# End of an edge stage: pieces of the node chunks placed by tables of steps, two edges' node rows fetched by SyncE

## The chip, the cores and the metric

The kernel runs on one core of one Trainium2 chip. The metric is the device time of one execution in microseconds (us). Engines are written as in the profile: PE (matrix multiplication, with PEld for its weight loads), DVE (VectorE), ACT (ScalarE), POOL (GpSimd) and SP (SyncE, here only an issuer of transfers).

## What is computed

Four graph layers over 1250 nodes with 512 features, each followed by a layer norm. The last one is the one that matters here; it is the only layer that reads an attribute for every one of the 21250 edges:

```python
msg = jax.nn.relu(x[src] + edge_attr)
agg = jax.ops.segment_sum(msg, dst, num_segments=x.shape[0])
h = x + agg
h = jax.nn.relu(h @ W1 + b1) @ W2 + b2
h = x + h
mean = h.mean(axis=0)
var = h.var(axis=0)
h = (h - mean) * jax.lax.rsqrt(var + BN_EPS) * gamma + beta
```

Edges are sorted by `dst`, so the sums of the first nodes are ready long before those of the last.

## The kernel before

**Groups.** The edge stage of the last layer works through 42 groups of 512 edges (`NG = 42`), four tiles of 128 edges each; the last group has 258 edges, so its tiles 2 and 3 hold one edge each. For a group g, SP loads the attributes into one of nine slots `ea`, and POOL gathers the node rows of the sources into one of three slots `xg` (`gather`, L490), one indirect transfer per tile, each of which waits until DVE has read that tile three groups earlier. DVE adds `xg` to `ea` (`add_rows`, L1020, four instructions) and writes the window matrix `hot_w` (L1023). ACT applies the relu (`rectify`, L657; L659 and L660 for the last group). PE multiplies (`scatter`, L1361, eight matmuls).

**Pairs.** Two groups make a pair m. After the second scatter ACT copies PSUM to `zn` (`evac_pair`, L667), PE transposes it (`turn`, L1371), and DVE adds four windows into the node sums `x3T` (`add_pair`, L1035). The places of the windows depend on the data: ahead of its wait for PE, `add_pair` loads four registers from SBUF (L1028).

**Chunks.** As soon as the pairs that touch a range of nodes are in, this range goes through the two matrix products. There are seven chunks q; chunks 2 to 4 are 180 nodes wide, 5 is 120 and 6 is 134. Each has four stages of four instructions or groups of 16 quarter pieces: `pre_chunk` on PE (L1382), `hidden_chunk` on ACT (L675), `out_chunk` on PE (L1393) and `add_chunk` on DVE (L1043, and bn_stats at L1046, which waits for L1043's semaphore). A piece is numbered 0 to 3, and pieces 0, 1 and 2, 3 are placed together as two halves. PSUM has two buffers for each product: `out_chunk` piece c waits until DVE has added piece c-2, and `pre_chunk` until ACT has read piece f-2. `hidden_chunk(q, 0)` waits until all of `out_chunk` of chunk q-1 is done, since `h1` has one buffer.

**Order.** Each engine runs its instructions strictly in the order of the program, and that order is written by a loop over steps g, one per group, that continues for `LATE = 9` steps behind the last group. In a step each engine does its work on group g, then the pair that is due, then the chunk pieces whose step it is, by `at_chunk(q)`, which is a number of steps behind the last group of the chunk. `pair_at(m)` is 2m+3 for m from 16 on, so pair 18 is added at step 39, pair 19 at 41, and pair 20, the last, at 43. Pieces of chunk 6 come last on all engines; its `pre_chunk` waits for every window of every pair. Behind it stand the statistics over all nodes, the normalisation and the last transposes and stores, which all need every chunk.

Of the kernel before, what the change touches and what calls it, by code (L numbers as in the profile page):

```python
# [27 lines left out]
P = 128  # L28
N = 1250
# [3 lines left out]
KC = D // P  # L33
NT = (N + P - 1) // P
# [22 lines left out]
FLAG_AT = 33  # L57
ACT_LOS = (2, 1, 2, 1)
NPAIR = NG // 2
LATE = 9  # L60
TURN_X = (18, 23)
GROUP_CUTS = (8, 16, 22, 28, 34, 38, NG)
GNODES, SLACK = 30, 24
NODE_CUTS = [0] + [GNODES * g - SLACK for g in GROUP_CUTS[:-1]] + [N]
NCUT = len(NODE_CUTS) - 1
SOON = 16
CMAX = max(b - a for a, b in zip(NODE_CUTS, NODE_CUTS[1:]))
XTILES = 4
TLAG = 3
# [1 line left out]
LN_SETS = ((0, 2), (2, 4), (4, 6), (6, 8), (8, 9), (9, 10))  # L71
PE_SUMS = (2, 3, 5, 6, 8, 9)
EPS = 1e-5
assert CS * (NCH - 1) + CH == N and NCODE <= 512 and NG == 2 + NT * HOTS and NG % 2 == 0 and NB * EW * 2 == P and not any(g % 2 for g in GROUP_CUTS)
assert BLOCK_SPAN * GE + 1 <= 4096 and BE < LAST < GE and (TPG * 2 + 3) * NG <= 512


# [4 lines left out]
def gnn_kernel(nc, x, src, dst, edge_attr, w01, b01, w02, b02, w11, b11, w12, b12, w2, b2,  # L82
               w31, b31, w32, b32, gamma, beta, out, x3_dram):
    with ExitStack() as ctx:
# [18 lines left out]
        def sem(name):  # L103
            return ctx.enter_context(nc.semaphore(name))
# [174 lines left out]
        ea_loaded = [sem(f"ea_loaded{i}") for i in range(RING)]  # L279
        xg_loaded = [[sem(f"xg_loaded{i}_{r}") for r in range(TPG)] for i in range(XRING)]  # L280
        idx_seen = sem("idx_seen")
        add_done, relu_done, win_ready = sem("add_done"), sem("relu_done"), sem("win_ready")
        scat_done, zn_ready, turn_done, win_added = sem("scat_done"), sem("zn_ready"), sem("turn_done"), sem("win_added")
        fix_x, fix_e, fix_msg, fix_done, fix_added = (sem("fix_x"), sem("fix_e"), sem("fix_msg"), sem("fix_done"), sem("fix_added"))
# [25 lines left out]

            return edge_attr[g * GE:(g + 1) * GE, :].rearrange("(b p r) d -> p b (r d)", b=NB, r=2)

        def at_chunk(q):

            return GROUP_CUTS[q] + (1 if NCUT - 3 <= q < NCUT - 1 else 3)

        def pair_at(m):

# [31 lines left out]
        def _(sp):  # L350
# [23 lines left out]
            def load(g):  # L374
                s = g % RING
                if g >= RING:
                    sp.wait_ge(scat_done, g - RING + 1)
                if g < NG - 1:
                    sp.dma_start(ea[s][:, :, :].rearrange("p (b r) d -> p b (r d)", b=NB), ea_rows(g)).then_inc(ea_loaded[s], 16)
                    return  # L380
                e0 = g * GE
                sp.dma_start(ea[s][:, 0:2, :].rearrange("p r d -> p (r d)"),
                             edge_attr[e0:e0 + BE, :].rearrange("(p r) d -> p (r d)", r=2)).then_inc(ea_loaded[s], 16)
                sp.dma_start(ea[s][0:LAST_P, 2:4, :].rearrange("p r d -> p (r d)"),
                             edge_attr[e0 + BE:e0 + BE + 2 * LAST_P, :].rearrange("(p r) d -> p (r d)", r=2)).then_inc(ea_loaded[s], 16)
# [7 lines left out]
            sp.wait_ge(y_done, 3 * NT)  # L393
            for g in range(early, NG):
                load(g)

            for j in range(NT):
                sp.wait_ge(x_ready, 3 * NT + j + 1)
# [6 lines left out]
        def _(pool):  # L405
# [77 lines left out]

            def gather(g):
                slot = g % XRING
                for r in range(TPG):
                    if g >= XRING:
                        pool.wait_ge(add_done, TPG * (g - XRING) + r + 1)
                    n = max(tile_rows(g, r), 2)
                    pool.indirect_dma_start(out=xg[0:n, slot, r, :], out_offset=None, in_=x3_dram[:, :],  # L490
                                            in_offset=bass.IndirectOffsetOnAxis(ap=srcT_i[0:n, r, g:g + 1], axis=0)).then_inc(xg_loaded[slot][r], 16)

            for g in range(NG):
                gather(g)
# [3 lines left out]
        def _(act):  # L498
# [170 lines left out]
            def hidden_chunk(q, f):  # L669

                n = NODE_CUTS[q + 1] - NODE_CUTS[q]
                act.wait_ge(pre_done, q * KC + f + 1)
                if q and f == 0:
                    act.wait_ge(h2_done, q * KC)
                act.activation(h1[:, f, 0:n], ps[:, 2 + f % 2, 0:n], ACT.Relu, bias=cols[:, 1, f:f + 1]).then_inc(h1_ready, 1)  # L675

            for g in range(NG + LATE):
                if g < NG:
                    rectify(g)
                if g % 2 == 0 and 2 <= g <= NG:  # L680
                    evac_pair(g // 2 - 1)
                for q in range(NCUT):
                    if g in (at_chunk(q) + 1, at_chunk(q) + 2):
                        for f in halves(g - at_chunk(q) - 1):
                            hidden_chunk(q, f)

            act.wait_ge(bn_step, 2 * KC)
            act.activation(bn_t[:, 0, :], bn_mv[:, :, 1:2].rearrange("p c a -> p (c a)"), ACT.Sqrt, bias=eps_s[:, 0:1]).then_inc(bn_sq, 1)
# [22 lines left out]
        def _(dve):  # L711
# [301 lines left out]
            def add_rows(g):  # L1013

                s, slot = g % RING, g % XRING
                dve.wait_ge(ea_loaded[s], 16 * (g // RING + 1) + 16 * (g == NG - 1))
                for r in range(TPG):
                    dve.wait_ge(xg_loaded[slot][r], 16 * (g // XRING + 1))
                    n = tile_rows(g, r)
                    dve.tensor_tensor(ea[s][0:n, r, :], ea[s][0:n, r, :], xg[0:n, slot, r, :], ALU.add).then_inc(add_done, 1)  # L1020
                if g >= RING:
                    dve.wait_ge(scat_done, g - RING + 1)
                dve.tensor_tensor(hot_w[:, s, :, :], iota_n[:, 0:EW].unsqueeze(1).to_broadcast([P, TPG, EW]),  # L1023
                                  relwT[:, :, g:g + 1].to_broadcast([P, TPG, EW]), ALU.is_equal).then_inc(win_ready, 1)
# [22 lines left out]
                if q == NCUT - 1:  # L1047
                    ins.then_inc(bn_step, 1)

            for g in range(NG + LATE):  # L1050
                if g < NG:
                    add_rows(g)
                for m in range(NPAIR):
                    if g == pair_at(m):
                        add_pair(m)
                for q in range(NCUT - 1):
                    if g in (at_chunk(q) + 5, at_chunk(q) + 7):
                        for cc in halves((g - at_chunk(q) - 5) // 2):
                            add_chunk(q, cc)

            for cc in range(KC):
                add_chunk(NCUT - 1, cc)
                dve.wait_ge(bn_step, 2 * cc + 1)
# [53 lines left out]
        def _(pe):  # L1117
# [276 lines left out]
                                    start=(k == 0), stop=(k == KC - 1))  # L1394
                ins.then_inc(h2_done, 1)

            for g in range(NG + LATE):
                if g < NG:
                    scatter(g)
                if g % 2 == 0 and 2 <= g <= NG:  # L1400
                    turn(g // 2 - 1)
                for q in range(NCUT):
                    if g in (at_chunk(q), at_chunk(q) + 1):
                        for f in halves(g - at_chunk(q)):
                            pre_chunk(q, f)
                    if g in (at_chunk(q) + 3, at_chunk(q) + 5):
                        for cc in halves((g - at_chunk(q) - 3) // 2):
                            out_chunk(q, cc)

            for j in range(NT):  # L1410
                for i, (n0, n1) in enumerate(BN_PARTS):
# [44 lines left out]
```

## Time and profile before

| | us |
|---|---|
| median of 3 runs | 590.97 |
| lowest, highest | 589.76, 594.39 |
| the profiled execution, time | 594.86 |
| the profiled execution, span from first to last instruction | 593.2 |
| PE busy | 495.4 (84%) |
| DVE busy | 395.8 (67%) |
| POOL busy | 302.5 (51%) |
| ACT busy | 251.9 (42%) |

The time of an execution is a little above its span (1.66 us here). Shares of busy time are averages over stages with different limits: the edge stage fills about the stretch from 310 to 560 us, and the change touches its last 35 us. Starts in the rows below are microseconds from the beginning of the span. In a timeline several like instructions that follow each other are one row (x16 is sixteen), and an idle time before a row stands in brackets with what ended it. PE's successive matmuls overlap a little, so the distance from one row's start to the next is slightly below the row's duration.

### The profile page before, as it was taken

What the parts mean: (1) busy time and instruction counts of PE and PEld (TensorE: products, weight loads), DVE (VectorE), ACT (ScalarE), POOL (GpSimd) and SP (SyncE); (2) the same over time, 40 slices, a digit from 0 to 9 for tenths busy, and PEclk for the clock granted to TensorE, in tenths of its full rate; (3) what the DMA queues carried; (4) which work ended last, traced back from release to release, by engine and by line L of the source; (5) the groups of instructions that cost most, each with busy time, mean ns of one, the idle gap of its engine ahead of it and who ended that gap; (6) DMA issues with size and microseconds to landing.
All of it is one profiled execution on the core that took longest, in us unless ns stands there. A gap on an engine that the chain in (4) does not pass through costs nothing.

```text
span 593.2 us, 7933 instructions
## 1 busy us (share of the span) xinstructions
PE 495.4 (84%) x2461; PEld 345.9 (58%) x2461; DVE 395.8 (67%) x894; ACT 251.9 (42%) x435; POOL 302.5 (51%) x328
## 2 busy tenths in 40 slices
PE   4999999999999998999992546578569876889875
PEld 2544459997899964899881101134235543465775
DVE  7999986768848959111672646565694776787375
ACT  7677751121285126410124424434435343444335
POOL 8999838301004005850004777777777777773000
PEclk9999999999999999999996567779979899899979
DMA  7900000000000400000947899999999999973004
GB/s 263 270 1 0 2 2 1 0 0 2 0 1 2 143 0 0 2 0 0 371 178 299 299 395 371 385 396 389 393 388 358 399 397 399 354 193 95 1 1 173
DMA packets 35604, 102.64 MB, mean 173 GB/s; under 512 B 6635, under 2 KB 7277, under 8 KB 35562
## 3 DMA queue, kind: packets, MB, share of 16 engines
q1 hardware_dynamic: 22150, 58.51, 26.4%
q0 software_dynamic: 13344, 43.53, 20.4%
q8 instruction: 20, 0.33, 0.2%
q14 instruction: 22, 0.18, 0.1%
q10 hardware_dynamic: 68, 0.09, 0.0%
HBM read 96.99 MB, written 5.12 MB: 172 GB/s over the span
## 4 chain that ended last, share of the span: by engine, by line
PE 42%; POOL 15%; DMA 14%; DVE 14%; issue 7%; ACT 5%; DVEq 3%; ACTq 0%; SPq 0%; POOLq 0%
DMA xg<-x_dram,srcT_i 13%; PE ps L1200 12%; POOL xg L490 11%; PE ps L1239 10%; PE ps L1212 7%; POOL hot_lo L426 4%; DVE ea L1020 3%; DVE hot_code L815 3%; PE ps L1268 2%; PE ps L1361 2%; PE ps L1382 2%; PE ps L1393 2%; ACT countsT L592 2%; DVEq L1028 2%; PE ps L1155 1%
## 5 line engine op out<-in xcount | busy, mean ns | idle before, releaser
L490 POOL DMA_INDIRECT xg<-x_dram,srcT_i x168 | 171.8, 1022 | 109.3 <-DMA x_dram<-xn 57.5
L1361 PE MATMUL ps<-ea,hot_w 128*32 128x512 f32 x336 | 94.5, 706 | 68.0 <-ACT ea L657 67.9
L1020 DVE TENSOR_TENSOR ea<-ea,xg 128x512 f32<-128x512 f32 x168 | 108.8, 689 | 35.1 <-DMA xg<-x_dram,srcT_i 34.7
L657 ACT ACTIVATE ea<-ea 128x2048 f32<-128x2048 f32 x41 | 78.3, 1910 | 110.3 <-DVE ea L1020 110.3
L1361 PEld LDWEIGHTS ps<-ea,hot_w 128*32 128x32 f32 x336 | 17.6, 120 | 123.5 <-ACT ea L657 72.9
L426 POOL TENSOR_SCALAR hot_lo<-iota_n,src_loT 128x128 bf16<-128x128 f16 x105 | 65.9, 644 | 4.8 <-PE ps L1155 3.9
L1035 DVE TENSOR_TENSOR x3T<-x3T,ps 128x128 f32 x84 | 24.3, 289 | 45.0 <-issue 26.0
L815 DVE TENSOR_SCALAR hot_code<-iota_c,codeT 128x380 bf16<-128x380 f16 x168 | 49.2, 352 | 2.4 <-issue 0.8
L1382 PEld LDWEIGHTS ps<-x3T,w_s 128*128 128x128 f32 x224 | 35.9, 200 | 9.6 <-issue 5.8
L1177 PE MATMUL ps<-w_s,xT 128*128 128x512 f32 (+1 forms) x80 | 41.1, 595 | 0.0
L1382 PE MATMUL ps<-x3T,w_s 128*128 128x180 f32 (+4 forms) x224 | 39.6, 332 | 1.1 <-ACT h L675 1.1
L1155 PE MATMUL ps<-hot_code,hot_lo 128*128 128x380 bf16 x168 | 35.9, 337 | 5.2 <-DVE hot_code L815 2.6
L1393 PE MATMUL ps<-h,w_s 128*128 128x180 f32 (+4 forms) x224 | 36.6, 318 | 0.8 <-ACT h L675 0.5
L1155 PEld LDWEIGHTS ps<-hot_code,hot_lo 128*128 128x128 bf16 x168 | 15.6, 100 | 34.3 <-DVE hot_code L815 19.0
L1393 PEld LDWEIGHTS ps<-h,w_s 128*128 128x128 f32 x224 | 33.7, 190 | 1.7 <-ACT h L675 0.7
L574 ACT ACTIVATE std<-mv,eps_s 128x1 f32<-128x1 f32 x30 | 8.8, 294 | 59.8 <-DVE mv L906 59.8
L1212 PE MATMUL ps<-counts,xs_lo 128*128 (+1 forms) x120 | 32.9, 355 | 1.3 <-POOL xs_lo L450 1.3
L1212 PE MATMUL ps<-counts,xs_hi 128*128 (+1 forms) x120 | 33.1, 357 | 0.0
L445 POOL TENSOR_TENSOR g_lo<-g_f,g_hi 128x256 fp32r<-128x256 f32 (+1 forms) x10 | 7.3, 734 | 49.3 <-ACT g_f L608 49.3
L971 DVE TENSOR_TENSOR z_lo<-ps,z_hi 128x418 f32 x12 | 6.6, 589 | 38.0 <-ACT z_hi L641 38.0
L450 POOL TENSOR_TENSOR xs_lo<-xs_f,xs_hi 128x512 fp32r<-128x512 f32 (+1 forms) x10 | 12.7, 1275 | 37.5 <-ACT xs_hi L630 37.5
L826 DVE TENSOR_TENSOR counts<-ps,counts 128x380 f32 x42 | 22.8, 543 | 3.0 <-PE ps L1155 2.7
(180 smaller groups left out, 950.6 us busy)
## 6 DMA issues: line engine op xcount, KB each, us to landing
ea<-in_edge_attr_dram SPq DMA_DIRECT2D x41, 1024.0 KB, 9.7
w_s<-in_L_gnn_W_dram SPq DMA_DIRECT2D x5, 1024.0 KB, 8.8
xg<-x_dram,srcT_i POOLq DMA_INDIRECT x168, 7.4
xn<-in_x_dram SPq DMA_DIRECT2D x3, 768.0 KB, 8.4
x_dram<-xn SPq DMA_DIRECT2D x9, 256.0 KB
out_dram<-xn SPq DMA_DIRECT2D x9, 256.0 KB
w_s<-in_L_gnn_W_dram SPq DMA_DIRECT2D x2, 512.0 KB, 11.5
b_b<-in_L_gnn_b_dram SPq DMA_DIRECT2D x3, 256.0 KB, 10.0
```

The lines of the kernel that those rows point to most:

```text
L426: ins = pool.tensor_scalar(hot_lo[:, slot, r, :], iota_n[:, 0:P], src_loT[:, r, g:g + 1], None, ALU.is_equal)
L490: pool.indirect_dma_start(out=xg[0:n, slot, r, :], out_offset=None, in_=x3_dram[:, :], in_offset=bass.IndirectOffsetOnAxis(ap=srcT_i[0:n, ...
L657: act.activation(ea[s][:, :, :], ea[s][:, :, :], ACT.Relu).then_inc(relu_done, 1)
L815: ins = dve.tensor_scalar(hot_code[:, slot, r, :], iota_c[:, :], codeT[:, r, g:g + 1], None, ALU.is_equal)
L1020: dve.tensor_tensor(ea[s][0:n, r, :], ea[s][0:n, r, :], xg[0:n, slot, r, :], ALU.add).then_inc(add_done, 1)
L1155: ins = pe.matmul(ps[:, 4 + slot, 0:NCODE], hot_lo[:, slot, r, :], hot_code[:, slot, r, :], start=(r == 0), stop=(r == TPG - 1))
L1200: ins = pe.matmul(ps[:, cc, 0:CH], part[0:rows(j), j, P * cc:P * cc + P], rhs[0:rows(j), j, n], start=(first and m == 0), stop=(last and m ...
L1212: ins = pe.matmul(ps[:, cc, 0:CH], part[0:rows(j), j, P * cc:P * cc + P], rhs[0:rows(j), j, n], start=(j == 0 and part is parts[0]), stop= ...
L1239: ins = pe.matmul(ps[0:rows(j), 4 + n % 2, :], act_t[:, k, P * j:P * j + rows(j)], w[:, k, :], start=(m == 0), stop=(m == len(pairs) - 1))
L1361: ins = pe.matmul(ps[at_w:at_w + EW, 4 + g // 2 % 2, :], hot_w[:, g % RING, 2 * b + r, :], ea[g % RING][:, 2 * b + r, :], start=(r == 0), ...
L1382: ins = pe.matmul(ps[:, 2 + f % 2, 0:n1 - n0], w31_s[:, k, P * f:P * f + P], x3T[:, k, n0:n1], start=(k == 0), stop=(k == KC - 1))
L1393: ins = pe.matmul(ps[:, cc % 2, 0:n], w32_s[:, k, P * cc:P * cc + P], h1[:, k, 0:n], start=(k == 0), stop=(k == KC - 1))
```

## The change

Four things are changed.

1. `at_chunk` and `LATE` go; tables of steps say at which step each half of chunks 0 to 5 runs on each engine. Chunk 6 runs behind the loop, on each engine. Compared step by step, PE's first product and ACT's pieces stay at the steps they had. PE's second product moves for chunk 4 from steps 38 and 40 to 37 and 39, and for chunk 5 from 42 and 44 to 41 and 42: its first half now stands ahead of the transposes of the last pair. DVE's sums move for chunk 3 (second half) from step 38 to 37, for chunk 4 from 40 and 42 to 39 and 41, where the second half now stands ahead of pair 19, and for chunk 5 the first half now stands ahead of the last pair, where it stood behind it.
2. In a PE step in which both occur, `out_chunk` now precedes `pre_chunk`.
3. In the last group, tiles 2 and 3 (one edge each) are no longer gathered by POOL. SP loads two registers with the source numbers, waits until DVE has read these tiles of group 38, and issues two transfers of one row each. This stands behind all attribute loads and ahead of the stores of the output.
4. DVE adds the last group's tiles in the order 2, 3, 0, 1.

```diff
-LATE = 9
+PRE_AT = ((11, 12), (19, 20), (25, 26), (31, 32), (35, 36), (39, 40))
+HIDDEN_AT = ((12, 13), (20, 21), (26, 27), (32, 33), (36, 37), (40, 41))
+OUT_AT = ((14, 16), (22, 24), (28, 30), (34, 36), (37, 39), (41, 42))
+ADD_AT = ((16, 18), (24, 26), (30, 32), (36, 37), (39, None))
-        def at_chunk(q):
-
-            return GROUP_CUTS[q] + (1 if NCUT - 3 <= q < NCUT - 1 else 3)
+        def pieces(steps, g):
+
+            return [(q, 2 * i + c) for q, at_step in enumerate(steps) for i in range(2) if at_step[i] == g for c in range(2)]
...
+            ends = [sp.value_load(srcT_i[0:1, r, NG - 1:NG], min_val=0, max_val=N - 1) for r in (2, 3)]
+            sp.wait_ge(x3_stored, 16 * NT)
+            for r, end in zip((2, 3), ends):
+                sp.wait_ge(add_done, TPG * (NG - 1 - XRING) + r + 1)
+                sp.dma_start(xg[0:1, (NG - 1) % XRING, r, :], x3_dram[bass.ds(end, 1), :]).then_inc(end_loaded[r - 2], 16)
...
-                for r in range(TPG):
+                for r in range(TPG if g < NG - 1 else 2):
...
-            for g in range(NG + LATE):
-                if g < NG:
-                    rectify(g)
-                if g % 2 == 0 and 2 <= g <= NG:
+            for g in range(NG):
+                rectify(g)
+                if g % 2 == 0 and g >= 2:
                     evac_pair(g // 2 - 1)
...
+                for q, f in pieces(HIDDEN_AT, g):
+                    hidden_chunk(q, f)
+            evac_pair(NPAIR - 1)
+            for f in range(KC):
+                hidden_chunk(NCUT - 1, f)
...
-                for r in range(TPG):
-                    dve.wait_ge(xg_loaded[slot][r], 16 * (g // XRING + 1))
+                for r in range(TPG) if g < NG - 1 else (2, 3, 0, 1):
+                    if g == NG - 1 and r >= 2:
+                        dve.wait_ge(end_loaded[r - 2], 16)
+                    else:
+                        dve.wait_ge(xg_loaded[slot][r], 16 * (g // XRING + 1))
...
-            for g in range(NG + LATE):
-                if g < NG:
-                    add_rows(g)
-                for m in range(NPAIR):
+            for g in range(NG):
+                add_rows(g)
+                if g == NG - 1:
+                    for cc in halves(1):
+                        add_chunk(NCUT - 3, cc)
+                for m in range(NPAIR - 1):
                     if g == pair_at(m):
                         add_pair(m)
...
+                for q, cc in pieces(ADD_AT, g):
+                    add_chunk(q, cc)
+            for cc in halves(0):
+                add_chunk(NCUT - 2, cc)
+            add_pair(NPAIR - 1)
+            for cc in halves(1):
+                add_chunk(NCUT - 2, cc)
             for cc in range(KC):
                 add_chunk(NCUT - 1, cc)
...
-            for g in range(NG + LATE):
+            for g in range(NG + 1):
                 if g < NG:
                     scatter(g)
-                if g % 2 == 0 and 2 <= g <= NG:
+                if g % 2 == 0 and g >= 2:
                     turn(g // 2 - 1)
...
+                for q, cc in pieces(OUT_AT, g):
+                    out_chunk(q, cc)
+                for q, f in pieces(PRE_AT, g):
+                    pre_chunk(q, f)
+            for f in range(KC):
+                pre_chunk(NCUT - 1, f)
+            for cc in range(KC):
+                out_chunk(NCUT - 1, cc)
```

## Rows read from the trace of the kernel before

**Rows 1.** The page's tenths in 40 slices: busy PE, granted clock, DMA.
```profile
PE   4999999999999998999992546578569876889875
...
PEclk9999999999999999999996567779979899899979
DMA  7900000000000400000947899999999999973004
```

**Rows 2.** Windows: busy time (count) of PE, PEld, DVE, ACT, POOL; clock, DMA share, GB/s.
```profile
500.00:505.00 5.00, 4.32 (x24) 2.81 (x24) 2.28 (x4) 2.15 (x2) 3.78 (x5) 1.00 1.03 399
...
531.00:560.20 29.20, 26.59 (x167) 17.98 (x167) 18.97 (x49) 13.25 (x17) 8.04 (x8) 1.00 0.24 68
```

**Rows 3.** Timeline of PE: start, us, engine, line, operation [idle before].
```profile
534.21 1.91 PE L1361 MATMUL ps<-ea,hot_w 128*32 128x512 f32 x8
536.58 1.91 PE L1361 MATMUL ps<-ea,hot_w 128*32 128x512 f32 x8 [0.46 <-ACT ea L657]
538.42 0.66 PE L1371 MATMUL ps<-ident,zn 128*128 128x128 f32 x4
538.91 2.61 PE L1393 MATMUL ps<-h,w_s 128*128 128x180 f32 x16
541.45 1.91 PE L1361 MATMUL ps<-ea,hot_w 128*32 128x512 f32 x8
543.29 2.04 PE L1382 MATMUL ps<-x3T,w_s 128*128 128x120 f32 x16
545.27 1.91 PE L1361 MATMUL ps<-ea,hot_w 128*32 128x512 f32 x8
...
550.72 2.04 PE L1382 MATMUL ps<-x3T,w_s 128*128 128x120 f32 x16 [0.51 <-ACT h L675]
552.84 1.91 PE L1361 MATMUL ps<-ea,hot_w 128*32 128x512 f32 x8
555.44 0.66 PE L1371 MATMUL ps<-ident,zn 128*128 128x128 f32 x4 [0.69 <-ACT zn L667]
555.93 1.94 PE L1393 MATMUL ps<-h,w_s 128*128 128x120 f32 x16
558.19 2.02 PE L1393 MATMUL ps<-h,w_s 128*128 128x120 f32 x16 [0.31 <-DVE hT L1043]
560.04 3.83 PE L1382 MATMUL ps<-x3T,w_s 128*128 128x134 f32 x32
```

**Rows 4.** Timeline of DVE in the same stretch.
```profile
539.22 1.55 DVE L1035 TENSOR_TENSOR x3T<-x3T,ps 128x128 f32 x4 [2.27 <-PE ps L1371]
540.69 2.49 DVE L1020 TENSOR_TENSOR ea<-ea,xg 128x512 f32<-128x512 f32 x4
...
543.30 0.40 DVE L1043 SCALAR_TENSOR_TENSOR hT<-ps,cols,hT 128x180 f32<-128x180 f32 x1
...
544.69 2.47 DVE L1020 TENSOR_TENSOR ea<-ea,xg 128x512 f32<-128x512 f32 x4
...
550.68 0.35 DVE L1046 BATCH_NORM_STATS2 bn_st<-hT 128x6 f32<-128x180 f32 x1
556.24 1.55 DVE L1035 TENSOR_TENSOR x3T<-x3T,ps 128x128 f32 x4 [5.21 <-PE ps L1371]
...
560.62 0.29 DVE L1046 BATCH_NORM_STATS2 bn_st<-hT 128x6 f32<-128x120 f32 x1
```

**Rows 5.** Timeline of ACT in the same stretch: the last relus.
```profile
543.22 1.91 ACT L657 ACTIVATE ea<-ea 128x2048 f32<-128x2048 f32 x1 [4.40 <-DVE ea L1020]
...
550.80 1.06 ACT L659 ACTIVATE ea<-ea 128x1024 f32<-128x1024 f32 x1
```

**Rows 6.** L1028 from 552 to 556.2 us, DVE's sequencer: ns min/median/max, starts.
```profile
L1028 DVEq TENSOR_LOAD <-base_i x2: 300/301/302, 551.9 to 552.6; - x2
L1028 DVEq FUSED_REGOPS  x2: 183/183/183, 552.3 to 552.9; - x2
```

**Rows 7.** Timeline of POOL: the last gather, of one edge.
```profile
540.31 0.87 POOL L490 DMA_INDIRECT xg<-x_dram,srcT_i  x1 [0.30 <-issue]
```

**Rows 8.** Gathers from 535 to 546 us: issue to landing.
```profile
DMA to landing us min/median/max: 2.1/3.5/3.9
```

**Rows 9.** Timeline of PE: two scatters behind an idle stretch.
```profile
512.77 4.86 PE L1361 MATMUL ps<-ea,hot_w 128*32 128x512 f32 x16 [2.39 <-ACT ea L657]
```

More of the change, by code:

```diff
@@ L73 @@
 EPS = 1e-5
-assert CS * (NCH - 1) + CH == N and NCODE <= 512 and NG == 2 + NT * HOTS and NG % 2 == 0 and NB * EW * 2 == P and not any(g % 2 for g in GROUP_CUTS)
+assert LAST_P == 1 and LAST_R == 0 and CS * (NCH - 1) + CH == N and NCODE <= 512 and NG == 2 + NT * HOTS and NG % 2 == 0 and NB * EW * 2 == P and not any(g % 2 for g in GROUP_CUTS)
 assert BLOCK_SPAN * GE + 1 <= 4096 and BE < LAST < GE and (TPG * 2 + 3) * NG <= 512
@@ L281, in gnn_kernel @@
         idx_seen = sem("idx_seen")
+        end_loaded = [sem(f"end_loaded{i}") for i in range(2)]
         add_done, relu_done, win_ready = sem("add_done"), sem("relu_done"), sem("win_ready")
@@ L485, in gather @@
                 slot = g % XRING
-                for r in range(TPG):
+                for r in range(TPG if g < NG - 1 else 2):
                     if g >= XRING:
                         pool.wait_ge(add_done, TPG * (g - XRING) + r + 1)
-                    n = max(tile_rows(g, r), 2)
-                    pool.indirect_dma_start(out=xg[0:n, slot, r, :], out_offset=None, in_=x3_dram[:, :],
-                                            in_offset=bass.IndirectOffsetOnAxis(ap=srcT_i[0:n, r, g:g + 1], axis=0)).then_inc(xg_loaded[slot][r], 16)
+                    pool.indirect_dma_start(out=xg[:, slot, r, :], out_offset=None, in_=x3_dram[:, :],
+                                            in_offset=bass.IndirectOffsetOnAxis(ap=srcT_i[:, r, g:g + 1], axis=0)).then_inc(xg_loaded[slot][r], 16)
             for g in range(NG):
@@ L675, in hidden_chunk @@
                 act.activation(h1[:, f, 0:n], ps[:, 2 + f % 2, 0:n], ACT.Relu, bias=cols[:, 1, f:f + 1]).then_inc(h1_ready, 1)
-            for g in range(NG + LATE):
-                if g < NG:
-                    rectify(g)
-                if g % 2 == 0 and 2 <= g <= NG:
+            for g in range(NG):
+                rectify(g)
+                if g % 2 == 0 and g >= 2:
                     evac_pair(g // 2 - 1)
[L682 to L685, printed above, removed]
+                for q, f in pieces(HIDDEN_AT, g):
[3 more added lines that the diff above has]
+                hidden_chunk(NCUT - 1, f)
             act.wait_ge(bn_step, 2 * KC)
@@ L1048, in add_chunk @@
                     ins.then_inc(bn_step, 1)
-            for g in range(NG + LATE):
-                if g < NG:
-                    add_rows(g)
-                for m in range(NPAIR):
+            for g in range(NG):
[4 more added lines that the diff above has]
+                for m in range(NPAIR - 1):
                     if g == pair_at(m):
                         add_pair(m)
[L1056 to L1059, printed above, removed]
+                for q, cc in pieces(ADD_AT, g):
[5 more added lines that the diff above has]
+                add_chunk(NCUT - 2, cc)
             for cc in range(KC):
@@ L1395, in out_chunk @@
                 ins.then_inc(h2_done, 1)
-            for g in range(NG + LATE):
+            for g in range(NG + 1):
                 if g < NG:
                     scatter(g)
-                if g % 2 == 0 and 2 <= g <= NG:
+                if g % 2 == 0 and g >= 2:
                     turn(g // 2 - 1)
[L1402 to L1408, printed above, removed]
+                for q, cc in pieces(OUT_AT, g):
[6 more added lines that the diff above has]
+                out_chunk(NCUT - 1, cc)
             for j in range(NT):
```

## The prediction

> **What bounds the kernel now.** I read the page's slices first. PE is busy in eight or nine tenths of every slice but the first up to slice 21 (311 us); then comes the edge stage, where the DMA engines stand at nine tenths through slices 24 to 35 (341 to 519 us), PE at four to nine [rows 1]. So over most of the edge stage transfers set the pace, and the reader should see that this ends before the stage does: the DMA digit falls to 7, 3, 0, while PE's is 8, 9, 8. The change acts there. The windows give the two regimes in numbers: from 500 to 505 us the DMA engines are full (share 1.03), while from 531 to 560.2 us, with the clock at its higher level throughout, they are at 0.24 and PE is busy 26.59 of 29.20 us [rows 2]. The last 29 us of the stage are therefore bound by PE, and all that can be won there by any order of the same work is 29.20 - 26.59 = 2.6 us. The timeline of PE names these gaps: 0.46 us ahead of a scatter, 0.51 ahead of a first product, 0.69 for the copy of the last pair and 0.31 behind it [rows 3], and crumbs.
>
> Counting backwards, the scatters at 534.21, 536.58, 541.45, 545.27 and 552.84 are those of groups 37 to 41 [rows 3]. The end is set thus: the last scatter, the transposes of pair 20, both halves of chunk 5's second product, and chunk 6's first product at 560.04. Everything behind it (33 us) is a chain of its own that the change leaves as it is. So the question is one number: when does chunk 6's first product start? It needs PE to be free and the four window sums of pair 20, which now end at 556.24 + 1.55 = 557.8, 2.2 us early [rows 4].
>
> **The parts without a price.** (a) POOL's last gather is issued at 540.31 for 0.87 us, with 0.30 between gathers, and gathers land 2.1 to 3.9 us after issue [rows 7, 8]: by 545.1 us at the latest. DVE begins the last group's adds at 544.69 and needs the fourth tile three adds of about 0.62 us later, and then waits for nothing [rows 4]. Taking two gathers off POOL ends its work 2 x (0.87 + 0.30) = 2.3 us sooner, but it hides: the adds stand behind DVE's other work. I price it at 0; the bound on the gain is 2.3 us, if in some run the gathers were last. (b) SP has issued all attribute loads by then. It may fetch tile 2 when DVE has added tile 2 of group 38, about 534 us. With a gather's 3.9 us that is 538, nine us before the adds that I find below; 0, and only a fetch of over 12 us would cost. What stands behind it on SP are the output stores, 40 us later. (c) ACT's order is unchanged, and up to step 36 so is everybody's. (d) The new order of the last adds is the same work: 2.47 us [rows 4]. (e) Chunk 3's late sums move ahead of the adds of group 38 (1.4 us, the distance from 543.30 to 544.69 [rows 4]), which ACT at that time cannot take up sooner anyway.
>
> **The order replayed.** I take durations as the distances between starts in the rows, and keep the waits of the code. All in us. PE's scatter costs 1.84, its transposes 0.49, a half of the second product 2.54 at 180 nodes, and a half of the first at 120 nodes 1.98 [rows 3].
> - Scatter 37 stays at 534.21. Chunk 4's second product, first half, now follows at 536.05 and fills the gap of 0.46. Scatter 38: 538.59. Transposes of pair 18: 540.43, two us later than 538.42 before. Scatter 39: 540.92, and PE is free at 542.76.
> - DVE's sums of pair 18 follow the start of the transposes by 0.8 (539.22 - 538.42): 541.23 instead of 539.22. Behind them now stand the first sums of chunk 4, at 541.23 + 1.47 = 542.70 (1.47 is the distance 540.69 - 539.22), and only then group 40's adds, at 544.09 instead of 540.69 [rows 4]. This is the first cost: the adds of group 40 are 3.4 us later.
> - Chunk 4's second half on PE needs the buffer that DVE's first sum frees, 542.70 + 0.40 = 543.10; it starts at about 543.25 and ends at 545.79, having waited 0.5. The first half of chunk 5's first product: until 547.77.
> - Group 40's adds end at 544.09 + 2.49 = 546.58, its relu at 546.62 + 1.91 = 548.53 [rows 4, 5]. Scatter 40 starts at 548.58; PE has stood still for 0.8. Transposes at 550.42, chunk 5's first product, second half, from 550.91, and scatter 41 at 552.89. The relu of the last group is no hindrance: adds 546.74 to 549.21, relu from 549.6 to 551.6.
> So the last scatter starts at 552.89 where it started at 552.84. The gaps removed (0.46, 0.51, which was ACT waiting for chunk 4's second product) come back as 0.5 and 0.8.
>
> **Behind the last scatter.** Let T be the end of it, 554.73 (before: 554.68). Before, chunk 6 started at T + 5.36 [rows 3]. Now PE does chunk 5's first half at once, which hides the copy of the pair (0.69 saved), then the transposes, then the second half: PE is free at about T + 4.65, so PE alone would gain 0.7. But DVE has the half chunk's sums ahead of the last pair, and with them its register loads. Chunk 5's last bn_stats of a half starts 2.43 behind the start of that half's product (560.62 - 558.19 [rows 3, 4]). Then the loads: before, those of pair 20 began with the bn_stats ahead of them (550.68 [rows 4]) and the last began at 552.6, its register operation at 552.9 for 0.18 [rows 6]. Spacing 0.63, end 553.1, and some 0.15 to the first sum: 2.6 from that bn_stats' start to the first sum. Before, all of it lay in DVE's idle 5.21 us ahead of 556.24 [rows 4]; this cover is gone. First window sum at T + 2.43 + 2.6 = T + 5.05, the last ends 1.55 later [rows 4], T + 6.6, and chunk 6 starts at T + 6.7 = 561.4. That is 561.4 - 560.04 = +1.35. It is a wait of 2 us of PE, in place of one of 0.69 and one of 0.31.
>
> Could the loads run earlier? The bound below is that they are done in time: chunk 6 at T + 4.65 = 559.4, -0.65. The rows speak for the upper value: the loads of pair 20 began with the bn_stats that waits on a semaphore, not before, though DVE had idled. The Trainium skill (Advanced Engine Details and Errata, Engine Queue Depths) gives VectorE a queue of 8 instructions; if that let the four loads pass the four queued instructions of the half chunk, which wait for PE, the cost would vanish and the sum would be the -0.65 above. The trace does not agree for a queue headed by a wait.
>
> **Sum.** 0 for POOL, SP and ACT, +0.05 up to the last scatter, +1.3 behind it: +1.35. Against the profiled execution's own 594.86 this is 596.2. That execution lies above the median of the three runs; the same addition to the median gives 590.97 + 1.35 = 592.3.
>
> **Rivals.**
> - *DVE is ahead (faster).* The loads are hidden (-0.65), and the two new gaps of 0.5 and 0.8 shrink, since they hang on DVE too. All together -0.65 - 1.3 = -1.95: 589.0. For it: DVE idles 2.27 and 5.21 us in this stretch [rows 4], so the work fits. Against: the order of the program. It decides where the loads are done by T + 2.9, when the pair's transposes are. Chance 0.25.
> - *The clock falls (slower).* At about 512 us PE had idled 2.39 us, and two scatters took 4.86 where two distances of 1.84 are 3.7 [rows 9, 3]: +1.2. If the new gap of 2 us ahead of chunk 6 does the same, its price is at least this 1.2 and at most a doubling of the 3.83 of chunk 6's first product. 592.3 + 1.2 to 3.8: 593.5 to 596.1. Against: the gap is shorter. The Trainium skill (TensorE: Matmul & The Clock Gate, Why this matters for your kernels) advises against idle gaps between bursts of matmuls and names one longer than mine as harmful; by it nothing is added here. No row shows a fall behind a gap of 2 us. Chance 0.12.
> - *Nothing shows.* The moved work and the gather's 2.3 cancel, within 0.5 of before: 591.0. Chance 0.12.
> - *SP's fetch is late.* Place: DVE's first adds of group 41. It decides from 12 us of fetch on, three times what rows 8 show. Price: what exceeds it, shared with nothing: 593 and more. Chance 0.03.
>
> **How the numbers follow.** The forecast has 0.48 and its own range is 591.3 to 593.7 (each distance in the replay is good to about 0.1, some ten of them, and the load time to 0.5). The bounds above take the range to 588.8 (the faster rival) and 595.8 (most of the clock's). One per cent is 5.9 us, about what a measurement of this kernel can tell from no change; no case but sums of mishaps gets there, and the largest conceivable gain is 2.6 from PE's gaps and 2.3 from POOL. Faster by over 1%: 0.04, within: 0.91, slower: 0.05; what is not in the cases above I put there.
>
> **What would show it.** In the timeline of PE the order from 536 on: L1393 directly behind scatter 37, no 0.46; a gap of about 0.8 ahead of a scatter, ended by ACT's relu; and one of 1.5 to 2 ahead of the L1382 x32, ended by DVE's L1035. On DVE: L1028's last loads behind the L1046 of 120 nodes, and group 40's adds behind L1043. POOL: two gathers fewer, DVE without a wait for transfers in the last group. The prediction is wrong if chunk 6's first product starts without a gap, if its distance to the last scatter is below 7 us (before: 7.2), or if PE shows more than about 4 us of gaps between 531 and the start of chunk 6.

## The result, and the profile after

| | before | changed |
|---|---|---|
| median of 13 runs, us | 592.50 | 596.15 |
| lowest, us | 589.76 | 592.51 |
| ratio to before (95% interval) | | 1.0045 (1.0025 to 1.0065) |
| the profiled execution, time, us | 594.86 | 594.07 |
| its span, us | 593.2 | 592.4 |

The change costs 0.45% of 592.5, or 2.7 us (1.5 to 3.9). The ratio leaves out executions more than 1.5% above the fastest of the same kernel, here one of 2575.59 us of the changed kernel, whose cause no run shows. The sign is the forecast one and the size is twice the 1.35 us forecast. The median of 596.15 counts that one execution; over the other twelve it is 595.39. The kernel before, too, measures 1.5 us higher in 13 runs than in the three on which the prediction stood; on the median of those three the ratio gives 593.6.

The two profiled executions hide the loss: the changed one is even 0.8 us shorter. They differ ahead of the changed stretch, where the transfers of the edge stage set the pace (368 and 383 GB/s before, 374 and 391 now, in the windows from 330 to 400 and 400 to 460 us), so they have to be laid over each other at a mark behind that part. I use the second half of chunk 4's first product, the last one on 180 nodes (531.58 before, 528.46 now), and call the distance from it the *distance*. The timeline of PE in the changed kernel:

```profile
528.46 2.71 PE L1398 MATMUL ps<-x3T,w_s 128*128 128x180 f32 x16 [0.56 <-ACT h L684]
531.10 1.91 PE L1377 MATMUL ps<-ea,hot_w 128*32 128x512 f32 x8
532.94 2.71 PE L1409 MATMUL ps<-h,w_s 128*128 128x180 f32 x16
535.57 1.91 PE L1377 MATMUL ps<-ea,hot_w 128*32 128x512 f32 x8
...
540.23 2.68 PE L1409 MATMUL ps<-h,w_s 128*128 128x180 f32 x16 [0.31 <-DVE hT L1055]
542.74 1.94 PE L1398 MATMUL ps<-x3T,w_s 128*128 128x120 f32 x16
545.54 1.91 PE L1377 MATMUL ps<-ea,hot_w 128*32 128x512 f32 x8 [0.86 <-ACT ea L666]
...
549.75 1.91 PE L1377 MATMUL ps<-ea,hot_w 128*32 128x512 f32 x8
551.59 2.04 PE L1409 MATMUL ps<-h,w_s 128*128 128x120 f32 x16
553.48 0.60 PE L1387 MATMUL ps<-ident,zn 128*128 128x128 f32 x4
553.91 1.94 PE L1409 MATMUL ps<-h,w_s 128*128 128x120 f32 x16
558.33 5.59 PE L1398 MATMUL ps<-x3T,w_s 128*128 128x134 f32 x32 [2.47 <-DVE x3T L1047]
```

Against [rows 3] the reader should see three things. The small gaps have changed places: 0.46 and 0.51 are gone, 0.31 and 0.86 are there instead, and the last scatter stands at distance 21.29 where it stood at 21.26. Behind it PE runs without a gap for three pieces and then stands still for 2.47 us until DVE's sums of the last pair (L1047) are in; chunk 6 starts at distance 29.87 instead of 28.46. And the same 32 matmuls of chunk 6 then take 5.59 us instead of 3.83.

The timeline of DVE for the same end, from pair 18's sums (538.21) on; group 40's adds are at 541.06:

```profile
538.21 1.55 DVE L1047 TENSOR_TENSOR x3T<-x3T,ps 128x128 f32 x4 [4.20 <-PE ps L1387]
...
541.06 2.48 DVE L1032 TENSOR_TENSOR ea<-ea,xg 128x512 f32<-128x512 f32 x4
...
550.05 1.56 DVE L1047 TENSOR_TENSOR x3T<-x3T,ps 128x128 f32 x4 [2.32 <-issue]
552.78 0.34 DVE L1055 SCALAR_TENSOR_TENSOR hT<-ps,cols,hT 128x120 f32<-128x120 f32 x1 [1.18 <-PE ps L1409]
...
553.68 0.34 DVE L1055 SCALAR_TENSOR_TENSOR hT<-ps,cols,hT 128x120 f32<-128x120 f32 x1 [0.23 <-PE ps L1409]
554.05 0.29 DVE L1058 BATCH_NORM_STATS2 bn_st<-hT 128x6 f32<-128x120 f32 x1
556.72 1.55 DVE L1047 TENSOR_TENSOR x3T<-x3T,ps 128x128 f32 x4 [2.38 <-issue]
```

and the register loads of the last pair, on DVE's sequencer, with their first and last start:

```profile
L1040 DVEq TENSOR_LOAD <-base_i x4: 301/301/308, 554.1 to 555.9; - x4
L1040 DVEq FUSED_REGOPS  x4: 183/186/190, 554.4 to 556.3; - x4
```

DVE's idle 2.38 us ahead of the window sums waits for no engine: the profile calls it "issue", and the loads fill it, from the start of bn_stats at 554.05 on. The pair's transposes had been done at 554.1. Pair 19's sums at 550.05 stand behind four exposed loads as well (2.32 us), and PE shows no gap for it: DVE's next sums wait 1.18 us for PE anyway. Before, the four sums waited 5.21 us for PE, and the loads lay in that time [rows 4, 6].

### The profile page after: what moved, and what is told of

It is laid out like the page before. It is cut to its first block, busy times and chain, and to the rows that moved or that the text cites. A ratio compares the mean times of both kernels' runs of the same rounds, so it can differ in the third digit from the quotient of the medians.

```text
span 592.4 us, 7946 instructions
## 1 busy us (share of the span) xinstructions
PE 493.2 (83%) x2461; PEld 344.1 (58%) x2461; DVE 395.2 (67%) x894; ACT 251.6 (42%) x435; POOL 299.8 (51%) x326
## 4 chain that ended last, share of the span: by engine, by line
PE 42%; POOL 19%; DVE 14%; issue 10%; DMA 8%; ACT 4%; DVEq 2%; ACTq 0%
POOL xg L499 19%; PE ps L1216 12%; PE ps L1255 10%; DMA xg<-x_dram,srcT_i 7%; PE ps L1228 7%; DVE hot_code L824 5%; PE ps L1284 2%; PE ps L1398 2%; PE ps L1377 2%; ACT countsT L601 2%; DVE counts L835 2%; PE ps L1171 2%; PE ps L1409 1%; DVE stats L913 1%; DVE ea L1032 1%
## 5 line engine op out<-in xcount | busy, mean ns | idle before, releaser
L499 POOL DMA_INDIRECT xg<-x_dram,srcT_i x166 | 168.2, 1013 | 107.8 <-DMA x_dram<-xn 57.5
L1032 DVE TENSOR_TENSOR ea<-ea,xg 128x512 f32<-128x512 f32 (+1 forms) x168 | 108.7, 689 | 33.7 <-DMA xg<-x_dram,srcT_i 33.4
L1047 DVE TENSOR_TENSOR x3T<-x3T,ps 128x128 f32 x84 | 24.2, 288 | 46.3 <-issue 32.9
```

What stands on the lines that cost most here:

```text
L499: pool.indirect_dma_start(out=xg[:, slot, r, :], out_offset=None, in_=x3_dram[:, :], in_offset=bass.IndirectOffsetOnAxis(ap=srcT_i[:, r, g ...
```

## The experiments

All distances come from one profiled execution each; they repeat to 0.1 us as long as the product at the mark itself runs at the higher clock (2.71 us), while whole executions scatter by several. The kernels marked as having slower transfers ran beside a kernel before of 642 to 645 us, with wide intervals; the others beside one of 592 to 594 us. The last number of these two rows, GB/s in the edge stage, shows it, first for the changed kernel, then for the first of the slower ones. Ratios hold within a comparison. "Changed" was compared with the kernel before in a comparison of its own; the kernels from "loads early" to "busy gap" shared another.

```profile
400.00:460.00 60.00, 45.29 (x205) 23.61 (x205) 37.15 (x82) 26.37 (x23) 46.49 (x45) 0.94 1.02 391
```

```profile
400.00:460.00 60.00, 37.88 (x170) 21.40 (x168) 35.89 (x78) 19.74 (x18) 39.90 (x40) 0.82 0.93 340
```

| kernel | last scatter | chunk 6 starts | its first product takes | ratio (95%) |
|---|---|---|---|---|
| before | 21.26 | 28.46 | 3.83 | 1 |
| changed | 21.29 | 29.87 | 5.59 | 1.0045 (1.0025 to 1.0065) |
| loads early | 21.29 | 27.38 | 3.92 | 0.9951 (0.9927 to 0.9974) |
| chunk 5 only | 21.28 | 29.85 | 3.92 | 1.0022 (1.0001 to 1.0043) |
| SP only | 21.27 | 28.46 | 3.83 | 0.9987 (0.9966 to 1.0007) |
| busy gap | 21.28 | 29.86 | 3.92 | 1.0006 (0.9985 to 1.0026) |
| loads and adds early, slower transfers | 20.37 | 26.45 | 3.92 | 0.9926 (0.9871 to 0.9981) |
| loads doubled, slower transfers | 21.30 | 32.32 | 5.58 | 1.0112 (1.0001 to 1.0223) |
| loads and adds early, third time | 20.35 | 26.44 | 3.92 | 0.9964 (0.9941 to 0.9987) |

The kernels that the table leaves out had a late mark or no ratio, or repeat a row; they follow in the text.

**The loads taken from under the wait.** `window_places(m)` is the four loads taken out of `add_pair`. The places of the last pair are loaded directly behind the last group's adds, the sums stay where the change has them:

```diff
             for g in range(NG):
                 add_rows(g)
                 if g == NG - 1:
+                    last_places = window_places(NPAIR - 1)
                     for cc in halves(1):
                         add_chunk(NCUT - 3, cc)
...
-            add_pair(NPAIR - 1)
+            add_pair(NPAIR - 1, last_places)
```

> The changed kernel, with the four register loads of the last pair taken from the pair's own place to a place directly behind the last group's adds, where 2.5 us of adds cover them. Theory A (the loads stand exposed between chunk 5's first sums and the last pair, and the gap they make lets the clock fall): the gap of 2.47 us ahead of chunk 6's first product goes to at most 0.3, that product takes 3.83 us instead of 5.59, the distance from chunk 4's last first-product half to chunk 6's start is 27.3 us (changed kernel 29.87, before 28.46), and the time is 0.996 to 1.000 of before. Theory B (the loss sits further up, in the adds of group 40 that stand behind pair 18): the gap closes but the time stays near 1.003. Theory C (the window sums themselves stand too late, not their loads): the gap stays above 1.5 us.

Its timeline of PE:

```profile
551.33 1.91 PE L1382 MATMUL ps<-ea,hot_w 128*32 128x512 f32 x8
553.17 2.04 PE L1414 MATMUL ps<-h,w_s 128*128 128x120 f32 x16
555.06 0.60 PE L1392 MATMUL ps<-ident,zn 128*128 128x128 f32 x4
555.49 1.94 PE L1414 MATMUL ps<-h,w_s 128*128 128x120 f32 x16
557.42 3.92 PE L1403 MATMUL ps<-x3T,w_s 128*128 128x134 f32 x32
```

No gap, and full clock. Chunk 6 starts at 27.38 as expected, 2.49 us sooner than in the changed kernel and 1.08 sooner than before. Theories B and C fall: nothing but four loads was moved, and the kernel is faster than both, by a little more than I had expected (0.9951, where 0.996 was the end of my range; the interval holds it). Not all of it is explained: against the kernel before the ratio says 2.9 us (1.5 to 4.3), the distance only 1.08, and behind the start of chunk 6 this trace shows no gain. In the same trace the four loads start from 542.9 to 544.7 us, beside group 40's adds and ahead of the last group's adds (545.25), behind which they stand in the program.

**One part of the change alone.** In the kernel before, only chunk 5's first half goes ahead of the last pair:

```diff
-                    if g in (at_chunk(q) + 3, at_chunk(q) + 5):
+                    if g in (at_chunk(q) + (2 if q == NCUT - 2 else 3), at_chunk(q) + 5):
...
+                if g == pair_at(NPAIR - 1):
+                    for cc in halves(0):
+                        add_chunk(NCUT - 2, cc)
```

> The kernel before, with one thing of the change: the first half of chunk 5's second product ahead of the last pair's transposes on PE, and its sums ahead of the last pair's sums on DVE. All else is as before. Theory A: this alone makes a gap of 2 to 2.5 us ahead of chunk 6, whose start moves from 28.46 to 29.8 us behind chunk 4's last first-product half; +1.35 us without a fall of the clock, about +3.1 with one; time 1.002 to 1.005 of before. Theory B: 1.000, since the adds of group 40 are not delayed here.

```profile
550.18 1.91 PE L1364 MATMUL ps<-ea,hot_w 128*32 128x512 f32 x8
...
558.75 3.92 PE L1385 MATMUL ps<-x3T,w_s 128*128 128x134 f32 x32 [2.47 <-DVE x3T L1035]
```

The gap is there to the hundredth, 2.47 us, and chunk 6 starts at 29.85. So the whole shift comes from this one exchange, none of it from the tables for chunks 3 and 4 or from SP. But the product behind the gap took 3.92 us: in this execution the clock did not fall. The ratio, 1.0022, is the forecast's 1.35 us almost exactly (0.22% of 594 is 1.3), but its interval reaches from 0.1 to 2.6 us, so this closeness proves nothing, and it does not tell this kernel from the changed one.

**SP's rows alone.** The kernel before with points 3 and 4 of the change:

```diff
-                for r in range(TPG):
+                for r in range(TPG if g < NG - 1 else 2):
...
+                sp.dma_start(xg[0:1, (NG - 1) % XRING, r, :], x3_dram[bass.ds(end, 1), :]).then_inc(end_loaded[r - 2], 16)
```

> The kernel before, with only the other part of the change: tiles 2 and 3 of the last group fetched by SP, two gathers fewer on POOL, and the order 2, 3, 0, 1 of the last adds. Theory A: POOL ends 2.3 us sooner, nothing on PE, DVE or ACT moves by more than 0.2 us; 0.999 to 1.001 of before. Theory C' (the transfers matter): faster by up to 2.3 us, 0.996, or slower if DVE waits for SP's rows.

SP's two transfers and POOL's last gather, from the timelines of the two engines:

```profile
532.06 0.77 SPq L402 DMA_DIRECT2D xg<-x_dram  x2
...
536.37 0.95 POOL L496 DMA_INDIRECT xg<-x_dram,srcT_i  x1 [0.30 <-issue]
```

POOL is done at 537.3 instead of 541.2, by the mark 3.6 us sooner (2.3 had been expected), and no distance on PE moves by more than 0.01 us. The ratio 0.9987 can't be told from 1. This part is hidden, as forecast.

**The gap filled with useless work.** In the changed kernel, PE transposes the unit matrix into a free bank:

```diff
+            for i in range(12):
+                pe.transpose(ps[:, 5, 0:P], ident[:, :], ident[:, :])
             for f in range(KC):
                 pre_chunk(NCUT - 1, f)
```

> The changed kernel, with 12 transposes of the unit matrix into a PSUM bank that is free then, between chunk 5's last product and chunk 6's first: work that nobody needs, about 1.5 us, inside the gap of 2.47 us. If the fall of the clock is caused by the idle gap, chunk 6's first product takes 3.83 us instead of 5.59 at an unchanged start, and the time is 1.000 to 1.003 of before where the changed kernel has 1.0045. If the clock falls on its own account, the product stays at 5 us or more and the ratio at 1.0045.

```profile
556.97 1.47 PE L1423 MATMUL ps<-ident 128*128 128x128 f32 x12
559.60 3.92 PE L1398 MATMUL ps<-x3T,w_s 128*128 128x134 f32 x32 [1.16 <-DVE x3T L1047]
```

Chunk 6 starts at 29.86 as in the changed kernel, with 1.16 us of standstill instead of 2.47, and its product takes 3.92 us. The ratio is 1.0006 where the changed kernel has 1.0045, 2.3 us less. That fits a clock that falls because PE stands still, but it is not shown: the intervals touch (up to 1.0026, down from 1.0025), and the two ratios come from different comparisons. In this one the kernel with chunk 5's half alone has the same gap without the useless work; its 1.0022 can't be told from 1.0006, and its product took 3.92 us too.

**The adds of group 40 first.** DVE idles 4.20 us in the changed kernel ahead of pair 18's sums. Group 40's adds go there, and the places of the last three pairs are loaded early:

```diff
             for g in range(NG):
-                add_rows(g)
+                if g != NG - 2:
+                    add_rows(g)
+                if g == NG - 3:
+                    places[g // 2 - 1] = window_places(g // 2 - 1)
+                    add_rows(NG - 2)
                 if g == NG - 1:
+                    for m in (NPAIR - 2, NPAIR - 1):
+                        places[m] = window_places(m)
```

> The changed kernel with the loads of the last three pairs moved ahead, as in the early-loads kernel, and also group 40's adds ahead of pair 18's sums and chunk 4's first sums, into DVE's idle 4.2 us there. Theory A: the gap of 0.86 us ahead of scatter 40 goes as well; the last scatter starts 20.4 us behind chunk 4's last first-product half (before 21.26, changed 21.29, early loads 21.29), chunk 6's first product at 26.5 (28.46, 29.87, 27.38), the time is 0.995 to 0.998 of before, and below that of the early-loads kernel by about 0.9 us. Rival: the adds of group 40 wait for their gathers or delay pair 18, and nothing is won over the early-loads kernel.

The last scatter is at 20.37 and chunk 6 at 26.45, both as expected, two us ahead of before; the gap of 0.86 is gone. The ratio was 0.9926 with slower transfers. It ran twice more:

> The kernel with early loads and early adds again, since its first runs fell on a chip with slower transfers and gave a wide interval. Theory A: last scatter at 20.4 us, chunk 6 at 26.5 us behind chunk 4's last first-product half, no gap ahead of chunk 6, 0.993 to 0.998 of before. Rival: the early-loads kernel's 0.9951 was mostly luck of the clock, and this one comes to 0.998 or more.

0.9919 (0.9877 to 0.9961), distances 20.36 and 26.45, transfers slow again.

> The kernel with early loads and early adds a third time, to see its ratio where transfers are as fast as in the first comparison (before at about 592 us). Theory A: the distances are 20.4 and 26.5 us again, and the ratio is 0.993 to 0.997; on a chip with slower transfers (before at about 643 us) again 0.992 with a wide interval.

```profile
544.47 1.91 PE L1388 MATMUL ps<-ea,hot_w 128*32 128x512 f32 x8
...
548.67 1.91 PE L1388 MATMUL ps<-ea,hot_w 128*32 128x512 f32 x8
...
554.76 3.92 PE L1409 MATMUL ps<-x3T,w_s 128*128 128x134 f32 x32
```

0.9964 with the fast transfers: 2.1 us (0.8 to 3.5) below before, 4.8 below the changed kernel by the two ratios, which come from two comparisons. That it is also faster than the kernel with early loads alone (0.9951) is not shown; the 0.9 us between them are visible in the distances, not in the times.

**The loads doubled.** In the changed kernel the four loads ahead of the last pair are done twice:

```diff
+            for j in range(4):
+                dve.value_load(base_i[0:1, 1 + j % NB, NG - 2 + j // NB:NG - 2 + j // NB + 1], min_val=0, max_val=N - EW)
             add_pair(NPAIR - 1)
```

> The changed kernel with the four register loads ahead of the last pair's sums done twice, the first time for nobody. If the gap ahead of chunk 6 consists of these loads, it goes from 2.47 us to 5.0, chunk 6 starts at 32.4 us behind chunk 4's last first-product half (changed kernel 29.87), and the time is 1.007 to 1.012 of before. If the loads lie beside something else that ends later, the gap grows by less than 2 us.

```profile
608.83 5.58 PE L1400 MATMUL ps<-x3T,w_s 128*128 128x134 f32 x32 [4.92 <-DVE x3T L1047]
```

The gap grows from 2.47 to 4.92 us: four loads cost 2.45 us, 0.61 each. Nothing else lies beside them. The ratio, 1.0112 (1.0001 to 1.0223), lies in the expected range and is too wide to say more.

**Does the clock fall behind every such gap?** Two traces for that question alone, both with slower transfers.

> The changed kernel once more, for its trace alone. The gap ahead of chunk 6 is 2.47 us again; open is whether the clock falls behind it, as in the first trace of the changed kernel (product 5.59 us), or not, as in the kernel with chunk 5's half alone, which has the same gap (3.92 us). If each gap of this length brings a fall, 5.6; if it depends on where the gap lies, either.

> The kernel with chunk 5's half alone once more, for its trace alone: the same question, the same gap of 2.47 us. If the fall depends on the gap alone, both kernels show the same in each trace, which the first traces already speak against; if it depends on chance, traces of one kernel differ.

The changed kernel shows 2.47 and 5.52 us again. Chunk 5 alone, which kept its clock the first time, now shows 2.48 and 5.59. So it is not the kernel that decides; traces of one kernel differ. Nor is it the length of the gap alone. With slower transfers PE also stands still ahead of the product at the mark, and in the changed kernel's second trace it looks like this:

```profile
574.49 2.71 PE L1398 MATMUL ps<-x3T,w_s 128*128 128x180 f32 x16 [2.81 <-ACT h L684]
```

A gap of 2.81 us, and the product at full speed. In the five traces with 2.8 to 3.0 us there, four have 2.71 us (gaps of 2.81, 2.97, 2.97 and 3.01) and one has 4.38 (2.92). What decides stays open.

**The adds alone, and POOL's gathers in the fast version.** Both with slower transfers. First the adds alone:

```diff
             for g in range(NG):
-                add_rows(g)
+                if g != NG - 2:
+                    add_rows(g)
+                if g == NG - 3:
+                    add_rows(NG - 2)
```

> The changed kernel with group 40's adds ahead of pair 18's sums, the loads left where the change puts them. Theory A: the gap of 0.86 us ahead of scatter 40 is gone and the last scatter starts at 20.4 us (changed 21.29), but the gap ahead of chunk 6 stays at 2.47 us, chunk 6 starts at 29.0 us (changed 29.87, before 28.46), and the time is 1.001 to 1.004 of before. Rival: the middle of the schedule sets the time, and this alone brings it to 0.999 or less.

The distances came out at 22.03 and 30.60, not 20.4 and 29.0. The cause stands at the mark itself:

```profile
576.01 4.38 PE L1401 MATMUL ps<-x3T,w_s 128*128 128x180 f32 x16 [2.92 <-ACT h L684]
...
584.80 1.91 PE L1380 MATMUL ps<-ea,hot_w 128*32 128x512 f32 x8
...
598.04 1.91 PE L1380 MATMUL ps<-ea,hot_w 128*32 128x512 f32 x8
...
606.61 5.59 PE L1401 MATMUL ps<-x3T,w_s 128*128 128x134 f32 x32 [2.47 <-DVE x3T L1047]
```

With slow transfers PE had idled 2.92 us ahead of the mark, and the product at the mark ran 4.38 us instead of 2.71. From the scatter of group 38 on the picture is clean: 598.04 - 584.80 = 13.24 us to the last scatter, 14.18 in the changed kernel (549.75 - 535.57). The adds are worth 0.94 us, as expected, and the gap ahead of chunk 6 stays 2.47. The ratio, 0.9985 (0.9939 to 1.0030), decides nothing.

The other kernel is the fast version with tiles 2 and 3 of the last group gathered by POOL again; SP's two transfers and the new order of the last adds are taken out too:

```diff
-                for r in range(TPG if g < NG - 1 else 2):
+                for r in range(TPG):
```

> The kernel with early loads and early adds, but tiles 2 and 3 of the last group gathered by POOL again and added in their old order. Theory A (SP's part is worth nothing): the same distances, 20.4 and 26.5 us, and the same time as the version with SP within 0.3%. Rival: with the adds earlier, the last gathers now end last, the last group's adds wait for them, and the last scatter starts 1 us later or more.

```profile
574.33 5.17 PE L1402 MATMUL ps<-x3T,w_s 128*128 128x180 f32 x16 [3.61 <-ACT h L679]
...
584.38 1.91 PE L1381 MATMUL ps<-ea,hot_w 128*32 128x512 f32 x8
...
597.62 1.91 PE L1381 MATMUL ps<-ea,hot_w 128*32 128x512 f32 x8
```

Its mark is slow too (distances 23.29 and 29.38). From scatter 38 to the last scatter it takes 597.62 - 584.38 = 13.24 us, the very same as with SP's rows. The ratio 0.9965 (0.9916 to 1.0013) overlaps that of its partner in the same comparison. So in the schedule SP's part is worth nothing even with the adds early.

## Why the prediction was right, and where its size was off

**The bound.** Right: the stretch was PE's, and the transfers did not matter in it. With slower transfers too, the distances of the changed kernel came out the same to 0.01 us (21.29 and 29.87). In three traces of other kernels they came out longer (chunk 5 alone again, the adds alone, POOL's gathers): there the product at the mark had itself run slow, with a granted clock of 0.50 to 0.60.

**Up to the last scatter.** Forecast +0.05, measured +0.03. The two gaps that replace the old ones were forecast as 0.5 and 0.8 and are 0.31 and 0.86. The delay of group 40's adds (forecast 3.4 us, 541.06 + 3.12 - 540.69 = 3.5 measured) is real and is paid by PE only with the 0.86, and by the adds-only kernel it can be had back.

**POOL, SP, ACT at nothing.** Right, by the kernel with SP's part alone and by the last comparison. My bound of 2.3 us for the case of late gathers was reached nowhere, not even with slower transfers.

**The loads.** Right in place and size: forecast 2.6 us from the start of bn_stats to the first sum, measured 556.72 - 554.05 = 2.67; chunk 6 forecast 1.35 us later, measured 1.41. Doubling them and moving them both say so. What I put against it, that DVE's queue might let the loads pass, did not happen. The Trainium skill (Advanced Engine Details and Errata, Engine Queue Depths) gives the depth of 8 and is not contradicted, but a queue's depth doesn't tell what may run ahead: behind an instruction whose semaphore was still open, the loads did not start (554.1 against a bn_stats at 554.05), while in the kernel with early loads they ran ahead of adds queued with nothing left to wait for. In this program each wait is an instruction of its own; whether the wait or the instruction behind it holds the loads was not separated.

**The faster rival's bound** was too small. I had -0.65 for hidden loads; the kernel with early loads shows -1.08, since PE's three pieces behind the last scatter take 4.25 us (557.42 - 553.17) and not my 4.65: behind each other they need less than the distances in [rows 3], which contain waits.

**The term that was mis-sized is the clock.** The sum of +1.35 took nothing for it, and the rival got 0.12. In the windows of the changed kernel (columns as in [rows 2]) the standstill and what follows it read:

```profile
555.90:558.30 2.40, 0.00 (x0) 0.00 (x0) 1.18 (x5) 0.00 (x0) 0.00 (x0) 1.00 0.00 0
...
558.30:561.70 3.40, 3.37 (x17) 3.38 (x18) 1.04 (x4) 0.37 (x1) 0.00 (x0) 0.58 0.01 2
```

Granted clock 1.00 while PE stood still and 0.58 on the mean of the row behind: most of it at the lower of the two levels, 1.2 GHz. It cost 5.59 - 3.83 = 1.76 us (1.67 against the 3.92 that the product takes behind the same gap at full clock), inside the 1.2 to 3.8 that the rival had. Of the five profiled executions with a gap of 2.47 or 2.48 us four show it (5.59, 5.52, 5.59, 5.59) and one doesn't (3.92); behind 4.92 us it fell, behind 1.16 us it did not. So 0.12 was too low for this place. The Trainium skill (TensorE: Matmul & The Clock Gate, Why this matters for your kernels) names a longer idle gap as harmful; here the measurement decides, and a shorter one can be enough. I had a row that said so, a fall behind 2.39 us [rows 9], and let the page and the word "shorter" outweigh it; besides, I had put the gap at 2 us where 2.47 was coming, by the same 0.4 us as in the paragraph above. The same trace had more to count than this one row. From 330 to 530 us it shows six standstills of PE between 2.2 and 3.0 us: behind two the clock is low (2.58 and 2.39), behind four it is not (2.73, 2.27, 2.95 and 2.42), as here:

```profile
500.68 1.91 PE L1361 MATMUL ps<-ea,hot_w 128*32 128x512 f32 x8 [2.42 <-ACT ea L657]
```

Two in six would have been the chance to write down; at chunk 6 it came out as four in five. How often it falls in executions without a profile is not known, so how much of the measured 2.7 us is the clock is not known either: the delay of 1.41 us lies just below the interval of 1.5 to 3.9.

**Adding up.** 1.41 for the gap and 1.76 for the clock make 3.17 at the start of chunk 6's second product (distance 35.92 against 32.75). At the end of the span the difference is 63.94 - 61.62 = 2.32. The last 28 us differ by 0.85 in the other direction, without any change in them, and over the other kernels with fast transfers that last part scatters from 27.7 to 29.1. The timelines show where. Both kernels stand still for 3.53 us ahead of the transposes of the last stage, and from chunk 6's second product to their start both take 7.45 us. Below, the first row has the first of these transposes and the second row two later ones, the same in both kernels; first before, then changed:

```profile
571.78 1.94 PE L1425 MATMUL ps<-ident,hT 128*128 128x128 f32 x8 [3.53 <-ACT hT L693]
...
577.35 0.39 PE L1422 MATMUL ps<-ident,hT 128*128 128x128 f32 x2
```

```profile
571.83 1.34 PE L1442 MATMUL ps<-ident,hT 128*128 128x128 f32 x8 [3.53 <-ACT hT L702]
...
576.59 0.39 PE L1439 MATMUL ps<-ident,hT 128*128 128x128 f32 x2
```

That is 5.57 us before and 4.76 in the changed kernel, 0.81 of the 0.85. In between two transposes take 0.63 us where they later take 0.39, and the granted clock was 0.50 from 572 to 575 us before. So it is another fall of the clock. It comes behind this standstill in every one of the fourteen traces (0.50 to 0.72 over the 4 us from the first transpose) and lasts longer in one execution than in another; what sets its length no experiment isolates. The measured 2.7 us lie between 2.32 and 3.17.

## What to carry to other kernels

A register load on an engine's sequencer costs nothing while that engine waits for something later anyway, and its whole 0.6 us when an instruction that waits for a semaphore is put ahead of it and the work behind it is what the next engine waits for: when work is moved ahead of a data-dependent step, load the addresses first, in the shadow of a long run of arithmetic. Filling a hole on one engine can dig a larger one on another, so follow each moved piece into the queue of the engine that ends last. And a standstill of TensorE is to be priced with the slower matmuls behind it, which, in the executions where the clock fell, cost more (1.76 us) than the delay of the start did (1.41).

## What I had not expected of the hardware

- A standstill of 2.47 us lowered the granted clock in four of five profiled executions, and the same kernel shows both; a product of 3.83 us then took 5.5 to 5.6. Elsewhere longer ones left it alone: 2.8 to 3.0 us ahead of the mark in four of five. With twelve useless transposes (1.47 us) within the standstill the clock stayed up, in the one execution seen.
- Register loads on DVE's sequencer ran ahead of adds that were queued and free to run (loads from 542.9 us, adds from 545.25), but not ahead of a bn_stats that waited (554.1 against 554.05).
- Three pieces of PE behind each other took 4.25 us where the sum of distances taken from a timeline with waits gave 4.65.
- The speed of transfers in the edge stage can differ between comparisons, which were run on different chips and at different times: 323, 340 and 306 GB/s against 374, 391 and 394 in the same three windows (330 to 400, 400 to 460 and 460 to 500 us), and with it the whole kernel by 8 to 9%.
